# A fused adaLN block on Trainium2: in the gradient loop, upstream products are issued one batch further ahead, the slope precedes the key rates on GpSimd, and a learning rate moves from the values to the hidden product

## The chip, the cores and the metric

The kernel runs on one core of a Trainium2 chip. The metric is the device time of one launch in microseconds (us), the median of several runs. The engines are named as the profile names them: PE is TensorE (matmuls), DVE is VectorE, ACT is ScalarE, POOL is GpSimd, SP is SyncE (it only issues DMAs here). Each engine works through its own list of instructions in order; engines wait for one another on semaphores.

## The reference

One block computes, for 8 batches of 256 tokens with 256 channels (2 heads of 128), a modulated layer norm, a fast-weight attention, a residual, a second modulated layer norm, a mixture of experts and a residual. The change lies in the fast-weight attention, where each batch and head gets three gradients:

```python
qkv = silu(x @ w_qkv.T);  q, k, v = ...       # per head 256 x 128, q and k normalised
lr  = softplus(x @ w_lr.T + BASE_LR_INV)      # three rates per token and head: lr0, lr1, lr2

gate_before_act   = w0 @ kT
hidden_before_mul = w2 @ kT
silu_gate = silu(gate_before_act)
hidden    = silu_gate * hidden_before_mul
dhidden   = w1.T @ vT
dhidden_before_mul = dhidden * silu_gate
dgate = dhidden * hidden_before_mul
dgate_before_act = _silu_backprop(dgate, gate_before_act)
dw1 = vT @ (hidden.T * lr1)
dw0 = dgate_before_act @ (k * lr0)
dw2 = dhidden_before_mul @ (k * lr2)
w0, w1, w2 = zeropower(dw0) + dw0, ...        # five Newton-Schulz steps in bf16 on all 48 matrices,
                                              # each divided by its Frobenius norm first
```

## The kernel before

The program is written by hand for each engine; the order of the work is the order of the code, and every dependence is a semaphore. Its stages, by the time of the profiled execution: layer norm, QKV and normalisation of the keys (0 to 72 us), the gradient loop (72 to 118), five Newton-Schulz steps over 12 groups of four matrices (to about 197), the output of the attention batch by batch (to about 255), and the mixture of experts (to the end).

**The gradient loop** runs over b = 0 to 7 (one batch each; a batch has two token tiles, so with two heads four 128x128 blocks). Per batch:

- PE, `fast_up(b)`: the upstream products. Four times a 128x256 product `kT` with `w0` and `w2` (names `w,kT`) and a 128x128 product `vT` with `w1` (`w1s,vT`), into PSUM banks that alternate with the parity of b. It ends with `up_ps`. For b >= 2 it waits for `b_dg` of batch b - 2.
- ACT, `sigmoid(b)`: sigmoid of the gate, tile `s_` (two buffers). `scaled_values(b)`: four 128x128 products of the values with their rate lr1, tile `vl1` (two buffers).
- DVE, `gate_slopes(b)`: `sg` = gate * sigmoid, `u` = (sigmoid - 1) * sg. `gate_products(b)`: `hid` = sg * hidden, `dhb` = sg * dhidden, two buffers each. `sg` and `u` have one buffer.
- POOL, `gate_slope(b)`: `u` = sigmoid - u, the slope (semaphore `b_ds`). `key_rates(b)`: four products that scale the keys by lr0 and lr2 (`kl0`, `kl2`, two buffers).
- DVE: `dgb` = u * hidden, then times dhidden (`b_dg`).
- PE, `grads(b)`: twelve 128x128 products into banks 6 and 7, which have no second buffer: it waits for `dw_sb`, the copies of the gradients of b - 1 out of these banks. Ends with `dw_ps`.
- ACT, `grads_out(b)`: two copies of 128x384 from PSUM to `dw` (`dw_sb`).
- DVE, `cast_grads(b)`: `dw` to bf16, tile `X` (`xb_ok`). ACT, `grad_squares(b)`: six squared sums of `X` (128x128 each, name `junk`). PE, `frob_sums(b)`: one small product that adds them over the partitions. ACT, `sum_out(b)`: copies the result to `fsum`. POOL, `frobenius`: root of it (`fnb`), two batches at a time at first.

In front of `frob_sums` and `grads`, PE waits for the `dw_sb` and the `f_sum` of the step before. After the loop come `x_init` (division by the norm), the first transposes (`first_turn` on PE, `first_turned` on ACT and DVE), the inverse norms of batches 4 and 5, the cast of batch 7 and its squares `gsq` on DVE, and then the first `Br` of the Newton-Schulz loop. ACT closes the loop with the squares of batches 5 and 6, the sums, and the copy of batch 7.

Of the kernel before, what the change touches and what calls it, by code (L numbers as in the profile page):

```python
# [27 lines left out]
P = 128  # L28
# [46 lines left out]
def build(nc, x_d, c_d, wmod_d, qkvw_d, w02_d, w1_d, wnat_d, wo_d, onw_d, gate_d, ident_d, moew_d, comb_d, out_d):  # L75
    ctx = ExitStack()
    with ctx:
# [74 lines left out]
        qkvlo = at("qkvlo", [P, KC, QKV + NLR], F32R, R_dw + 8 * KC * L * 2)  # L152
        names = [(f"{n}{i}", [P, 4, P], F32) for i in range(2) for n in ("s_", "hid", "dhb", "dgb", "kl0", "kl2", "vl1")]
        tb, end = carve(R_tmp, names + [("sg", [P, 4, P], F32), ("u", [P, 4, P], F32)])
        assert end <= R_wo
        s_sb, hid, dhb, dgb, kl0, kl2, vl1 = ([tb[i], tb[7 + i]] for i in range(7))
        sg, u = tb[14], tb[15]
        gsq = at("gsq", [P, 6, P], F32, R_tmp + 14 * 2048)
# [73 lines left out]
        def bank(i):  # L232
            return banks[i // 2][:, (i % 2) * BLK:(i % 2 + 1) * BLK]
# [11 lines left out]

            "up_ps", "sig", "b_sg", "b_u", "b_ds", "b_t", "b_dg", "b_kl", "b_vl", "dw_ps", "dw_sb",
            "xb_ok", "f_ss", "g_sq", "f_s7",
# [163 lines left out]
        def _(po):  # L411
# [90 lines left out]
            for b in range(1, B):  # L502
                if b == (NBLK - 1) * 4 // TPB:
                    po.wait_ge(S["sc_l"], 4 * NH)
                key_rates(b)
                gate_slope(b)
                if b == 5:
                    frobenius(0, 1)
# [88 lines left out]
        def _(ac):  # L597
# [41 lines left out]

            def scaled_values(b):  # L640
                for t in range(b * TPB, (b + 1) * TPB):
                    for h in range(NH):
                        ac.activation(vl1[b % 2][:, (t - b * TPB) * NH + h, :], v[:, h, t, :], ACT.Copy,
                                      scale=lr[:, t, 3 * h + 1:3 * h + 2]).then_inc(S["b_vl"], 1)

            def sigmoid(b):
# [52 lines left out]
            turned_q(NBLK - 1)  # L699
            ac.wait_ge(S["lr_ok"], 1)  # L700
            scaled_values(0)

# [23 lines left out]

            for b in range(B):
                if b >= 1:
                    sigmoid(b)
                if b >= 2:  # L730
                    ac.wait_ge(S["dw_ps"], b - 1)
                if b >= 1:
                    scaled_values(b)
                if b >= 2:
                    grad_squares(b - 2, range(6) if b < B - 1 else range(3))
                if b >= 1:
                    grads_out(b - 1)
                if b >= 3:
                    sum_out(b - 3)
# [133 lines left out]
        def _(pe_):  # L873
# [126 lines left out]
            def grads(b):  # L1000
                i = b % 2
                pe_.wait_ge(S["b_dg"], b + 1)
                pe_.wait_ge(S["b_vl"], 4 * (b + 1))
                if b >= 1:
                    pe_.wait_ge(S["dw_sb"], NH * b)
                else:
                    pe_.wait_ge(S["at_sb_q"], 2 * NH)
                for h in range(NH):
                    pe_.wait_ge(S["b_kl"], 4 * b + 2 * (h + 1))
                    if b == B - 1 and h == 1:  # L1010
                        frob_sums(B - 3)
                    for j, (left, right) in enumerate(((dgb, kl0), (vl1, hid), (dhb, kl2))):
                        for tl in range(TPB):
                            last = mm(bank(6 + h)[:, j * P:(j + 1) * P], left[i][:, tl * NH + h, :], right[i][:, tl * NH + h, :],  # L1014
                                      start=(tl == 0), stop=(tl == TPB - 1))
                last.then_inc(S["dw_ps"], 1)
# [21 lines left out]
            for b in range(1, B + 1):  # L1038
                if b < B and b > 1:
                    fast_up(b)  # L1040
                if b >= 3:
                    pe_.wait_ge(S["dw_sb"], NH * (b - 1))
                    if b >= 4:
                        pe_.wait_ge(S["f_sum"], b - 3)
                    if b < B:
                        frob_sums(b - 3)
                grads(b - 1)
# [240 lines left out]
        def _(ve):  # L1288
# [77 lines left out]
            def gate_slopes(b):  # L1366

                i = b % 2
                ve.wait_ge(S["sig"], b + 1)
                if b >= 2:  # L1370
                    ve.wait_ge(S["dw_ps"], b - 1)
                if b >= 1:
# [5 lines left out]
            def gate_products(b):  # L1378

                i = b % 2  # L1380
                ve.tensor_tensor(hid[i][:, :, :], sg[:, :, :], hid_ps(i), ALU.mult)
                ve.tensor_tensor(dhb[i][:, :, :], sg[:, :, :], dh_ps(i), ALU.mult)
# [51 lines left out]
            for b in range(B):  # L1434
                i = b % 2
                if b >= 1:
                    gate_slopes(b)
                    gate_products(b)
                ve.wait_ge(S["b_ds"], b + 1)
                ve.tensor_tensor(dgb[i][:, :, :], u[:, :, :], hid_ps(i), ALU.mult).then_inc(S["b_t"], 1)  # L1440
                ve.wait_ge(S["b_t"], b + 1)
                ve.tensor_tensor(dgb[i][:, :, :], dgb[i][:, :, :], dh_ps(i), ALU.mult).then_inc(S["b_dg"], 1)
                if b >= 1:
                    cast_grads(b - 1)
            for b in range(3):
# [289 lines left out]
```

## Time and profile before

| what | value |
|---|---|
| median of 3 runs | 679.16 us (678.9 to 680.42) |
| profiled execution, its own time | 679.29 us |
| span of that execution, first to last instruction | 677.5 us |
| PE busy in the span | 651.7 us (96%) |
| DVE, ACT, POOL busy | 467.4, 339.2, 229.6 us |
| gradient loop | 72 to 118 us |

A timeline row below gives the start in us from the span's beginning, the duration in us, the engine, the line of the program, the operation, the tile written and the tiles read (buffer numbers left out), the shapes, and how many instructions were merged into it. A bracket at the end says how long the engine stood idle before it and which instruction ended that wait. A duration includes the time until the result is written; the next instruction on the engine may start a little earlier, so costs on an engine are taken from start to start.

### The profile page before, as it was taken

To read this page: it belongs to the slowest core of one execution; us is meant where nothing else is said; L and a number is where in the kernel's file an instruction comes from. 1 tells how busy PE (TensorE), PEld (TensorE's weight loads), DVE (VectorE), ACT (ScalarE), POOL (GpSimd) and SP (SyncE) were. 2 spreads that over 40 slices of the span, in tenths; PEclk is the share of its full clock that TensorE was granted. 3 is DMA by queue.
4 is the path that set the end of the run, shared out by engine and by line. 5 is a ranking of instruction groups with operands and counts; after the bars stand their busy time and mean duration, and the time that the engine had idled before them with its cause. 6 is when DMAs were issued, how large, how long until landed. Compare 5 with 4: busy or idle time off the path is not lost.

```text
span 677.5 us, 11548 instructions
## 1 busy us (share of the span) xinstructions
PE 651.7 (96%) x4146; PEld 560.6 (83%) x4146; DVE 467.4 (69%) x921; ACT 339.2 (50%) x725; POOL 229.6 (34%) x221
## 2 busy tenths in 40 slices
PE   7999998799988999999999999999999999999997
PEld 7889898799976887878888888888888888888885
DVE  6988878889977787774457665667556665555545
ACT  4788699789988855533222223322223332222331
POOL 4578868868177631340003310133002330000000
PEclk7999999999999999999999999999999999999999
DMA  8000000150000000430023422233222331122122
GB/s 327 6 1 1 1 2 3 46 174 26 3 2 0 2 1 1 121 104 25 15 86 108 107 75 69 78 117 109 63 66 86 109 117 67 62 66 69 54 94 107
DMA packets 23095, 43.58 MB, mean 64 GB/s; under 512 B 3544, under 2 KB 5856, under 8 KB 22912
## 3 DMA queue, kind: packets, MB, share of 16 engines
q1 hardware_dynamic: 22624, 42.26, 19.8%
q8 instruction: 34, 0.56, 0.4%
q10 hardware_dynamic: 416, 0.59, 0.3%
q14 instruction: 21, 0.17, 0.1%
HBM read 40.60 MB, written 2.24 MB: 63 GB/s over the span
## 4 chain that ended last, share of the span: by engine, by line
PE 78%; DVE 9%; POOL 6%; ACT 4%; issue 2%; DMA 1%; DVEq 0%; SPq 0%; ACTq 0%; POOLq 0%
PE ps L1176 40%; PE ps L1261 20%; PE ps L973 3%; PE ps L1100 2%; PE ps L1124 2%; PE ps L1111 2%; PE ps L1125 2%; PE ps L1140 2%; PE ps L1014 1%; PE ps L1222 1%; DVE x L1625 1%; PE ps L1198 1%; POOL qk L446 1%; ACT junk L725 1%; DMA x<-in_x 1%
## 5 line engine op out<-in xcount | busy, mean ns | idle before, releaser
L866 ACT ACTIVATE sgm<-ps,zero 128x512 f32<-128x512 f32 x100 | 69.0, 691 | 272.9 <-PE ps L1176 272.8
L1676 DVE TENSOR_TENSOR am<-sgm,ps 128x512 f32<-128x512 f32 x88 | 60.6, 689 | 138.9 <-ACT sgm L866 138.8
L1176 PE MATMUL ps<-h2hi,whi 128*128 128x512 f32 x400 | 156.1, 390 | 0.0
L1176 PE MATMUL ps<-h2lo,whi 128*128 128x512 f32 x400 | 155.6, 389 | 0.0
L1176 PE MATMUL ps<-h2hi,wlo 128*128 128x512 f32 x400 | 155.6, 389 | 0.0
L536 POOL CAST whi<-raw 128x768 fp32r<-128x768 f32 x25 | 23.2, 927 | 239.6 <-DMA raw<-in_moew 239.6
L1176 PEld LDWEIGHTS ps<-h2lo,whi 128*128 128x128 f32 x400 | 75.1, 188 | 15.7
L1176 PEld LDWEIGHTS ps<-h2hi,whi 128*128 128x128 f32 x400 | 75.1, 188 | 15.6
L1176 PEld LDWEIGHTS ps<-h2hi,wlo 128*128 128x128 f32 x400 | 75.1, 188 | 15.4
L1261 PE MATMUL ps<-ahi,whi 128*128 128x512 f32 x200 | 77.9, 390 | 0.1
L1261 PE MATMUL ps<-ahi,wlo 128*128 128x512 f32 x200 | 77.8, 389 | 0.0
L1261 PE MATMUL ps<-alo,whi 128*128 128x512 f32 x200 | 77.8, 389 | 0.0
L1640 DVE TENSOR_TENSOR alo<-pm,ahi 128x512 fp32r<-128x512 f32 x100 | 76.1, 761 | 0.2
L1685 DVE TENSOR_TENSOR pm<-am,cw 128x512 f32<-128x512 f32 x88 | 70.4, 800 | 5.3 <-DMA cw<-combine 2.9
L856 ACT ACTIVATE ahi<-pm 128x512 fp32r<-128x512 f32 x100 | 62.2, 622 | 2.0 <-DVE pm L1685 1.0
L538 POOL TENSOR_TENSOR wlo<-raw,whi 128x768 fp32r<-128x768 f32 x25 | 48.3, 1932 | 2.0
L1496 DVE SCALAR_TENSOR_TENSOR Br<-ps,Ar 128x512 bf16<-128x512 f32 x60 | 41.4, 691 | 6.6 <-PE ps L1111 5.6
L1261 PEld LDWEIGHTS ps<-ahi,whi 128*128 128x128 f32 x200 | 37.5, 188 | 8.3 <-DVE alo L1640 0.5
L1261 PEld LDWEIGHTS ps<-alo,whi 128*128 128x128 f32 x200 | 37.5, 188 | 7.8
L1261 PEld LDWEIGHTS ps<-ahi,wlo 128*128 128x128 f32 x200 | 37.5, 188 | 7.7
L764 ACT ACTIVATE Ar<-ps 128x512 bf16<-128x512 f32 x60 | 35.5, 594 | 5.5 <-DVE Br L1496 2.8
L772 ACT ACTIVATE X<-ps 128x512 bf16<-128x512 f32 x60 | 35.9, 599 | 2.3 <-PE ps L1125 0.5
(213 smaller groups left out, 1183.3 us busy)
## 6 DMA issues: line engine op xcount, KB each, us to landing
raw<-in_moew SPq DMA_DIRECT2D x25, 384.0 KB, 3.9
cw<-combine SPq DMA_DIRECT2D x32, 256.0 KB, 3.2
cw<-combine SPq DMA_DIRECT2D x16, 224.0 KB, 3.0
cw<-combine SPq DMA_DIRECT2D x16, 192.0 KB, 2.8
cw<-combine SPq DMA_DIRECT2D x16, 160.0 KB, 2.7
wog<-combine SPq DMA_DIRECT2D x2, 1024.0 KB, 6.3
cw<-combine SPq DMA_DIRECT2D x16, 128.0 KB, 3.0
out<-x1T SPq DMA_DIRECT2D x8, 256.0 KB, 3.6
```

The source lines that it names most:

```text
L536: po.tensor_copy(whi[wg % 2][:, c, :], raw[:, j % 2, :]).then_inc(S["w_hi"], 1)
L538: po.tensor_tensor(wlo[wg % 2][:, c, :], raw[:, j % 2, :], whi[wg % 2][:, c, :].bitcast(F32), ALU.subtract).then_inc(S["w_prep"], 1)
L764: ac.activation(Ar[:, n % 2, :], bank(n % 2), ACT.Copy, scale=NS[n // NGRP][1]).then_inc(S["a_sb"], 1)
L772: ac.activation(X[:, g * MPG:(g + 1) * MPG, :], bank(4 + n % 2).rearrange("p (a d) -> p a d", d=P), ACT.Copy).then_inc(S["x_sb"], 1)
L856: ac.activation(ahi[:, n % 4, :], pm[:, n % 3, :], ACT.Copy).then_inc(S["e_hi"], 1)
L866: ac.activation(sgm[:, n % 2, :], gate_bank(n), ACT.Silu, bias=zero[:, :]).then_inc(S["e_sg"], 1)
L1176: last = mm(o, w_, a_[:, kc, tok], start=(kc == 0 and k == 0), stop=(kc == KC - 1 and k == 2))
L1261: last = mm(bank(6 + f), w_, a_, start=(c == 0 and k == 0), stop=(c == CPG - 1 and k == 2))
L1496: ve.scalar_tensor_tensor(out=Br[:, n % 2, :], in0=bank(2 + n % 2), scalar=c_ / (b_ * b_), in1=Ar[:, n % 2, :], op0=ALU.mult, op1=ALU.add) ...
L1640: ve.tensor_tensor(alo[:, n % 3, :], pm[:, n % 3, :], ahi[:, n % 4, :].bitcast(F32), ALU.subtract).then_inc(S["e_lo"], 1)
L1676: ve.tensor_tensor(am[:, n % 2, :], sgm[:, n % 2, :], lin_bank(n), ALU.mult).then_inc(S["e_a"], 1)
L1685: ve.tensor_tensor(pm[:, n % 3, :], am[:, n % 2, :], cw[:, k % 3, :], ALU.mult).then_inc(S["e_p"], 1)
```

## The change

It does four things. (1) On PE, the loop issues `fast_up(b + 1)` ahead of `grads(b - 1)`, where it was `fast_up(b)`; so `fast_up(2)` stands ahead of `grads(0)`, and no upstream product is left in front of `grads(6)`. ACT takes the sigmoids a batch earlier in its list accordingly. (2) On POOL, from batch 1 on, `gate_slope(b)` stands ahead of `key_rates(b)`. (3) The rate lr1 is multiplied into `hid` on DVE: four 128x128 instructions with a rate per partition in place of one of 128x512. `scaled_values` and the tile `vl1` go away; PE reads the values `v` themselves. (4) On DVE the cast of a gradient moves: `cast_grads(b - 2)` between the products and `dgb` of batch b, in place of `cast_grads(b - 1)` behind them; the wait for the gradients of b - 2 moves from `sg` to `hid`.

```diff
@@ POOL @@
             for b in range(1, B):
                 if b == (NBLK - 1) * 4 // TPB:
                     po.wait_ge(S["sc_l"], 4 * NH)
+                gate_slope(b)
                 key_rates(b)
-                gate_slope(b)
@@ ACT @@
-            def scaled_values(b):
-                for t in range(b * TPB, (b + 1) * TPB):
-                    for h in range(NH):
-                        ac.activation(vl1[b % 2][:, (t - b * TPB) * NH + h, :], v[:, h, t, :], ACT.Copy,
-                                      scale=lr[:, t, 3 * h + 1:3 * h + 2]).then_inc(S["b_vl"], 1)
...
-            ac.wait_ge(S["lr_ok"], 1)
-            scaled_values(0)
+            sigmoid(1)
...
-            for b in range(B):
-                if b >= 1:
-                    sigmoid(b)
-                if b >= 2:
-                    ac.wait_ge(S["dw_ps"], b - 1)
-                if b >= 1:
-                    scaled_values(b)
+            for b in range(1, B):
+                if b + 1 < B:
+                    sigmoid(b + 1)
                 if b >= 2:
                     grad_squares(b - 2, range(6) if b < B - 1 else range(3))
                 if b >= 1:
@@ PE @@
                 pe_.wait_ge(S["b_dg"], b + 1)
-                pe_.wait_ge(S["b_vl"], 4 * (b + 1))
...
-                    for j, (left, right) in enumerate(((dgb, kl0), (vl1, hid), (dhb, kl2))):
+                    for j in range(3):
                         for tl in range(TPB):
-                            last = mm(bank(6 + h)[:, j * P:(j + 1) * P], left[i][:, tl * NH + h, :], right[i][:, tl * NH + h, :],
-                                      start=(tl == 0), stop=(tl == TPB - 1))
+                            m = tl * NH + h
+                            left, right = ((dgb[i][:, m, :], kl0[i][:, m, :]), (v[:, h, b * TPB + tl, :], hid[i][:, m, :]),
+                                           (dhb[i][:, m, :], kl2[i][:, m, :]))[j]
+                            last = mm(bank(6 + h)[:, j * P:(j + 1) * P], left, right, start=(tl == 0), stop=(tl == TPB - 1))
...
             for b in range(1, B + 1):
-                if b < B and b > 1:
-                    fast_up(b)
+                if b + 1 < B:
+                    fast_up(b + 1)
@@ DVE @@
                 ve.wait_ge(S["sig"], b + 1)
-                if b >= 2:
-                    ve.wait_ge(S["dw_ps"], b - 1)
...
-                ve.tensor_tensor(hid[i][:, :, :], sg[:, :, :], hid_ps(i), ALU.mult)
+                if b >= 2:
+                    ve.wait_ge(S["dw_ps"], b - 1)
+                if b == 0:
+                    ve.wait_ge(S["lr_ok"], 1)
+                for tl in range(TPB):
+                    for h in range(NH):
+                        m = tl * NH + h
+                        ve.scalar_tensor_tensor(out=hid[i][:, m, :], in0=hid_ps(i)[:, m, :],
+                                                scalar=lr[:, b * TPB + tl, 3 * h + 1:3 * h + 2], in1=sg[:, m, :], op0=ALU.mult, op1=ALU.mult)
...
                     gate_products(b)
+                if b >= 2:
+                    cast_grads(b - 2)
...
-                if b >= 1:
-                    cast_grads(b - 1)
+            cast_grads(B - 2)
```

The end of the loop on PE, behind the gradients of batch 5 (`kl`, `hid` and `dhb` of odd batches are numbered 88 to 92 before and 87 to 90 in the change, of even ones 81 to 85). Before, the upstream products of the last batch follow (two of eight rows shown):

```order
L1014 MATMUL ps<-kl_91,dgb_90 128x128 x2
L1014 MATMUL ps<-hid_88,vl_93 128x128 x2
L1014 MATMUL ps<-kl_92,dhb_89 128x128 x2
L942 MATMUL ps<-w_124,kT 128x256
L944 MATMUL ps<-w1s,vT 128x128
```

In the change:

```order
L1005 MATMUL ps<-kl_90,dgb_89 128x128 x2
L1005 MATMUL ps<-hid_87,v 128x128 x2
L1005 MATMUL ps<-kl_91,dhb_88 128x128 x2
L987 MATMUL ps<-fss,ones 128x6
L1005 MATMUL ps<-kl_84,dgb_83 128x128 x2
L1005 MATMUL ps<-hid_81,v 128x128 x2
```

The upstream products have moved ahead of the gradients of batch 5; behind these, the norm sum of batch 4 and the gradients of batch 6 follow at once.

One batch on DVE (batch 2, buffers `s_80`, `hid_81`, `dhb_82`, `dgb_83`), before:

```order
L1374 TENSOR_TENSOR sg<-s_80,ps 128x512
L1376 SCALAR_TENSOR_TENSOR u<-s_80,sg 128x512
L1381 TENSOR_TENSOR hid_81<-sg,ps 128x512
L1382 TENSOR_TENSOR dhb_82<-sg,ps 128x512
L1440 TENSOR_TENSOR dgb_83<-u,ps 128x512
L1442 TENSOR_TENSOR dgb_83<-dgb_83,ps 128x512
L1415 CAST X<-dw 128x768
```

and in the change:

```order
L1362 TENSOR_TENSOR sg<-s_80,ps 128x512
L1364 SCALAR_TENSOR_TENSOR u<-s_80,sg 128x512
L1376 SCALAR_TENSOR_TENSOR hid_81<-ps,lr,sg 128x128 x4
L1378 TENSOR_TENSOR dhb_82<-sg,ps 128x512
L1411 CAST X<-dw 128x768
L1438 TENSOR_TENSOR dgb_83<-u,ps 128x512
L1440 TENSOR_TENSOR dgb_83<-dgb_83,ps 128x512
```

`hid` has become four instructions, and the cast (now of the gradient two batches back) stands between the products and `dgb`.

## Rows read from the trace of the kernel before

**Rows 1.** Busy time by window: us, engines' busy us, PE clock, DMA

```profile
72.00:118.00 46.00, 41.69 (x319) 39.34 (x317) 37.56 (x61) 39.93 (x144) 36.05 (x44) 1.00 0.01 1
```

**Rows 2.** PE's timeline, batches 0 to 3: start, duration, instructions, idle before

```profile
74.66 0.68 PE L1014 MATMUL ps<-kl,dgb 128*128 128x128 f32 x4 [1.60 <-DVE dgb L1442]
...
77.41 0.60 PE L942 MATMUL ps<-w,kT 128*128 128x256 f32 x2
...
80.03 0.62 PE L1014 MATMUL ps<-kl,dgb 128*128 128x128 f32 x4
...
82.72 0.60 PE L942 MATMUL ps<-w,kT 128*128 128x256 f32 x2
...
86.18 0.69 PE L1014 MATMUL ps<-kl,dgb 128*128 128x128 f32 x4
...
91.58 0.36 PE L998 MATMUL ps<-fss,ones 128*128 128x6 f32 x2
91.85 0.68 PE L1014 MATMUL ps<-kl,dgb 128*128 128x128 f32 x4
```

**Rows 3.** PE's timeline at the loop's end

```profile
114.26 0.68 PE L1014 MATMUL ps<-kl,dgb 128*128 128x128 f32 x4 [1.90 <-DVE dgb L1442]
...
117.23 0.83 PE L1034 MATMUL ps<-identb,X 128*128 128x128 bf16 x12
```

**Rows 4.** DVE's timeline, from the rates to the first gradient product

```profile
71.78 0.26 DVE L1409 SCALAR_TENSOR_TENSOR lr<-lrp,lrz 128x96 f32<-128x96 f32 x1
71.96 0.68 DVE L1381 TENSOR_TENSOR hid<-sg,ps 128x512 f32<-128x512 f32 x1
...
73.87 0.69 DVE L1442 TENSOR_TENSOR dgb<-dgb,ps 128x512 f32<-128x512 f32 x1
```

**Rows 5.** Groups of DVE by form: busy us, mean ns of one

```profile
L1625 DVE SCALAR_TENSOR_TENSOR x<-ps,rr,x 128x256 f32<-128x256 f32 x32 | 13.7, 478 | 3.6 <-POOL rr L581 2.6 <-PE ps L1222 1.0
...
L1440 DVE TENSOR_TENSOR dgb<-u,ps 128x512 f32<-128x512 f32 x8 | 5.5, 688 | 3.2 <-POOL u L484 3.2
...
L1531 DVE TENSOR_TENSOR ex<-ps,mx 128x128 f32<-128x128 f32 x2 | 0.6, 291 | 0.1
```

**Rows 6.** DVE's timeline: four such instructions in a row, in the output stage

```profile
215.53 1.66 DVE L1625 SCALAR_TENSOR_TENSOR x<-ps,rr,x 128x256 f32<-128x256 f32 x4 [1.38 <-POOL rr L581]
```

**Rows 7.** DVE's timeline, batches 3, 4 and 6

```profile
91.45 0.56 DVE L1415 CAST X<-dw 128x768 bf16<-128x768 f32 x1 [0.74 <-ACT dw L717]
92.48 0.69 DVE L1374 TENSOR_TENSOR sg<-s,ps 128x512 f32<-128x512 f32 x1 [0.47 <-ACT s L651]
...
95.29 0.69 DVE L1440 TENSOR_TENSOR dgb<-u,ps 128x512 f32<-128x512 f32 x1 [0.20 <-POOL u L484]
...
109.16 0.77 DVE L1415 CAST X<-dw 128x768 bf16<-128x768 f32 x1
```

**Rows 8.** ACT's timeline: batch 4, and the sum of batch 5

```profile
91.76 0.69 ACT L651 ACTIVATE s<-ps,zero 128x512 f32<-128x512 f32 x1 [0.28 <-PE ps L944]
92.35 1.27 ACT L643 ACTIVATE vl<-v,lr 128x128 f32<-128x128 f32 x4
93.52 0.39 ACT L725 ACTIVATE junk<-X,zero 128x128 f32<-128x128 bf16 x1
...
96.56 0.85 ACT L717 ACTIVATE dw<-ps 128x384 f32<-128x384 f32 x2
97.30 0.17 ACT L705 ACTIVATE fsum<-ps 128x6 f32<-128x6 f32 x1
...
116.33 0.15 ACT L705 ACTIVATE fsum<-ps 128x6 f32<-128x6 f32 x1
```

**Rows 9.** POOL's timeline: the key rates of batch 4

```profile
89.22 2.34 POOL L478 TENSOR_TENSOR kl<-qk,lr 128x256 f32<-128x256 f32 x4
```

**Rows 10.** DVE's timeline: the last cast and the first Br

```profile
119.81 0.52 DVE L1415 CAST X<-dw 128x768 bf16<-128x768 f32 x1
...
122.73 0.67 DVE L1496 SCALAR_TENSOR_TENSOR Br<-ps,Ar 128x512 bf16<-128x512 f32 x1
```

More of the change, by code:

```diff
@@ L152, in build @@
         qkvlo = at("qkvlo", [P, KC, QKV + NLR], F32R, R_dw + 8 * KC * L * 2)
-        names = [(f"{n}{i}", [P, 4, P], F32) for i in range(2) for n in ("s_", "hid", "dhb", "dgb", "kl0", "kl2", "vl1")]
+        names = [(f"{n}{i}", [P, 4, P], F32) for i in range(2) for n in ("s_", "hid", "dhb", "dgb", "kl0", "kl2")]
         tb, end = carve(R_tmp, names + [("sg", [P, 4, P], F32), ("u", [P, 4, P], F32)])
         assert end <= R_wo
-        s_sb, hid, dhb, dgb, kl0, kl2, vl1 = ([tb[i], tb[7 + i]] for i in range(7))
-        sg, u = tb[14], tb[15]
+        s_sb, hid, dhb, dgb, kl0, kl2 = ([tb[i], tb[6 + i]] for i in range(6))
+        sg, u = tb[12], tb[13]
         gsq = at("gsq", [P, 6, P], F32, R_tmp + 14 * 2048)
@@ L244, in build @@
             "lr_z", "lr_e", "lr_c", "lr_ok",
-            "up_ps", "sig", "b_sg", "b_u", "b_ds", "b_t", "b_dg", "b_kl", "b_vl", "dw_ps", "dw_sb",
+            "up_ps", "sig", "b_sg", "b_u", "b_ds", "b_t", "b_dg", "b_kl", "dw_ps", "dw_sb",
             "xb_ok", "f_ss", "g_sq", "f_s7",
```

## The prediction

> **What bounds the kernel now.** I read busy time by window first, then the timelines of PE, DVE and ACT in the window that the change touches. Outside 72 to 118 us no instruction changes, and the stages behind the loop follow one another without a fixed appointment, so the change is worth what it moves the start of the Newton-Schulz loop. I date that by the first `Br` on DVE, 122.73 us [rows 10], since it is held up there by the casts and squares of the last batches.
>
> In the window PE is busy 41.69 of 46 us [rows 1], so at most 4.3 us can be had, and that only if PE never waits. Its waits are mainly two: 1.60 us ahead of the first gradients [rows 2] and 1.90 us ahead of the last [rows 3], both for `dgb` of that batch. Between them PE is nearly full: a batch without a wait (gradients, upstream products, norm sum) takes 86.18 to 91.85 = 5.67 us [rows 2], and 39.6 us lie between the start of the first gradients (74.66) and that of the last (114.26), which is 5.66 per batch. The middle of the loop therefore has almost nothing to give. DVE does wait in every batch (0.74 for the copy of the gradient, 0.47 for the sigmoid, 0.20 for the slope [rows 7]), but those waits lie behind PE's 5.67.
>
> **The change part by part.**
>
> *Rate into hid, the head of the loop.* Before, `hid` started at 71.96, before the rates were written; now it must wait for them: 71.78 + 0.26 = 72.04, so 0.08 us [rows 4]. Then four 128-column instructions with a rate per partition replace one of 512. The trace has the same form at 256 columns: 478 ns for one [rows 5], four in 1.66 us, so (1.66 - 0.478)/3 = 0.394 from start to start [rows 6]. A column costs (688 - 291)/384 = 1.03 ns [rows 5]; 128 fewer columns leave 0.262 from start to start and 0.346 for one alone. The lower end is the rates' own instruction, 96 columns without PSUM: its successor starts 0.18 later [rows 4], with 32 more columns 0.21. I take 0.262, the nearest form: four are 1.05 in place of 0.60 (`hid`, `dhb` and the first `dgb` take 1.91 together, the last 0.71 with the wait for its result [rows 4]), so +0.45 (bounds +0.24 and +0.78). `dgb` of batch 0, and with it PE's start, comes 0.53 later (0.32 to 0.86): 74.66 + 0.53 = 75.19. In later batches the 0.45 lies behind PE (below).
>
> *PE's order.* What is called a batch further ahead is in its waits only a swap: `fast_up(b + 1)` and `grads(b - 1)` both wait for `dgb` of b - 1. From 75.19: `fast_up(2)` 2.62 (77.41 to 80.03) and 0.06 for a start from idle (gradients 2.75 after a wait, 2.69 without), gradients of 0 2.69, up(3) and gradients of 1 5.31, to 85.87; three batches of 5.67, to 102.88; up(7) 2.62, to 105.50; sum 0.27 and gradients of 5 2.75, to 108.52 [rows 2]. That needs the others to keep up. DVE: `sg` to `dgb` 2.81 less the wait 0.20 and the old `hid` 0.60 [rows 7], plus 1.05, cast 0.56, twice `dgb` 1.44: 5.06 us, or 5.27 with the cast at 0.77 [rows 7]: under 5.67, and its waits for the sigmoid and the slope find them done, since the sigmoid comes a batch earlier and the slope's place in POOL's list ahead of the key rates lets it run under `hid` and `dhb`. ACT: sigmoid 0.59, squares 3.04, copies 0.74, sum 0.12 [rows 8], 4.5. POOL: 36.05 us in the window [rows 1] is 4.5 per batch. So PE is full from 75.19 to 108.52, and the middle gains what it waited there: 4.3 less 1.6 and 1.9, some 0.8 us in all.
>
> *Values' rate gone from ACT.* Four instructions, 92.35 to 93.52 = 1.17 us per batch [rows 8], eight batches. ACT is not the bound, so this is worth nothing by itself; it pays only by making ACT's 4.5 fit under 5.67.
>
> *The end of the loop.* Here the swap costs. Before, up(7) stood between the gradients of 5 and of 6 and covered ACT's copies out of banks 6 and 7, which have no second buffer. Now nothing stands there. ACT's list is sigmoid(7), six squares, copies of 5, sum. The sigmoid starts 0.18 after PE leaves the products (91.58 to 91.76 [rows 2, 8]): 105.68; squares from 106.27 to 109.31; copies to 110.05; sum 0.17; PE goes on at about 110.3 (0.1 for the handover). It has waited 1.8 us. Sum and gradients of 6 to 113.3; copies from 113.47 to 114.21, sum, PE at 114.48: another 1.2 us, where before it was 1.90 for `dgb`. The gradients of 7 take 2.97 (114.26 to 117.23 [rows 3]), to 117.45, 0.2 later than before. ACT, free of copies at 114.33, still has three squares of batch 5 and three of 6 (1.52 each, half of 3.04) before the sum of batch 5: 117.37, where it was at 116.33 [rows 8]. Behind that sum hang the root on POOL, the inverse norms and, queued behind these on DVE, the cast of batch 7, its squares and the first `Br` [rows 10]. All of it moves by **+1.04 us** (0.83 to 1.37 with the bounds of `hid`).
>
> The sum is made against the profiled execution's own 679.29 us, of which 677.5 is span: 680.33. That execution lies 0.13 above the median of 679.16, so the median comes to **680.2**.
>
> *A rule weighed.* A cast on DVE and key rates on POOL disturb each other: 0.56 us in one place, 0.77 in another where POOL works [rows 7]. The Trainium skill (SBUF — State Buffer, "Who interferes with whom") says more: the two engines share a port pair as a lock, a cast can take it, and whoever comes second blocks until the other's whole instruction is done. In the change each cast lies over key rates. By the rows this adds 0.21 under PE's cover and nothing to the sum; by the rule as it stands a cast could lose a whole POOL instruction, which is the second rival; the rows so far show a third of one.
>
> **The rivals.**
>
> 1. *The forecast:* the middle gains 0.8, the head loses 0.53, the single-buffered banks give the rest back. 680.2, by its bounds 680.0 to 680.5.
>
> 2. *VectorE becomes the bound (slower).* `hid` at its upper end, 1.38, and each cast behind a whole key-rate instruction, 2.34/4 = 0.59 [rows 9]: 2.01 + 1.38 + 0.56 + 0.59 + 1.44 = 5.98 per batch against PE's 5.67. It decides from a DVE batch of 5.67 on. Six batches of 0.31 are 1.9, the head costs 0.33 more: 1.04 + 1.9 + 0.33 = +3.3, 682.4. For it: VectorE gets longer in a loop that is nearly full. Against: it takes both upper ends; one alone gives 5.39 or 5.65.
>
> 3. *VectorE alone sets what follows (faster).* It leaves the loop early: `hid` of batch 7 may start when the gradients of 5 are done (108.7); 1.05, 0.60, cast 0.56, `dgb` 1.44 give 112.3, where before PE got the last `dgb` at 114.26 [rows 3]. If the divisions by the norms could start then, all would come 1.9 earlier: 677.3. Against: the cast of batch 6 now stands ahead of them and waits for copies that end at 114.2.
>
> **How the numbers follow.** A measurement of this kernel can tell about 0.2% (1.36 us) from no change. The runs before spread over 1.5 us, so a median may be off by half a microsecond, beside the bounds of `hid` and of ACT's tail. The forecast gets 0.83: 0.58 within 0.2%, 0.24 above it, 0.01 below. VectorE as the bound gets 0.09 (slower), VectorE alone 0.08 (faster). So faster 0.09, same 0.58, slower 0.33. The range runs from 679.1 to 681.6: it holds the forecast's bounds with about a microsecond on either side, and leaves out both rivals and a little of the forecast's tails.
>
> **What would show it.** In the changed profile: PE's first upstream product of the loop after a wait at about 75.2; PE without a wait from there to about 108.5, a batch at 5.6 to 5.7; then two waits, about 1.8 and 1.2, ended by ACT's copy or sum and no longer by `dgb`; `hid` four at about 0.26 from start to start; DVE's waits now for the gradients' end ahead of `hid`; the first `Br` at about 123.8. The prediction is wrong if PE waits for `dgb` in the middle (rival 2), if the two late waits are missing or ACT's sum of batch 5 comes before 116.3 (rival 3), or if the `Br` moves and the end does not move with it.

## The result, and the profile after

The changed kernel takes 683.38 us (median of 15 runs, 679.98 to 685.0) against 680.83 us (15 runs of the kernel before, 677.73 to 682.88, taken beside them): a ratio of 1.0033, 95% interval 1.0021 to 1.0045, or +2.25 us (+1.4 to +3.1) by that ratio; the medians themselves lie 2.55 apart. In a second group of runs it was 682.13 against 680.43, ratio 1.0020 (1.0005 to 1.0034), +1.4 us. It is slower, the forecast of no measurable change was wrong, and 683.38 lies outside the range of 679.1 to 681.6.

The profiled execution of the changed kernel took 679.98 us, its fastest, with a span of 678.0. By the end of the span it would be only 0.5 us slower than the profile of before. That comparison is of no use here: from the first `Br` to the end, where no instruction differs, the two profiles of the kernel before took 554.8 and 557.3 us. Ahead of the loop the two executions differ as well, with no change there: from 8 to 16 us the granted clock of TensorE was 0.57 in the profile of before and 1.00 in that of the changed kernel. So I read everything from a point just ahead of the change to a point just behind it: from the start of the rates (the instruction that writes `lr` on DVE) to the first `Br`. The same measure is used for every kernel below.

Busy time by window (us, busy us of PE, weight loads, DVE, ACT, POOL, then PE's clock, DMA share, GB/s) of the kernel after; [rows 1] answer to the first line:

```profile
72.00:118.00 46.00, 40.86 (x300) 38.76 (x300) 39.93 (x82) 28.84 (x103) 35.12 (x43) 0.96 0.01 1
...
72.00:82.00 10.00, 7.77 (x45) 7.03 (x45) 8.36 (x18) 1.37 (x2) 5.98 (x10) 0.83 0.01 2
...
76.00:77.00 1.00, 1.00 (x4) 0.82 (x4) 1.00 (x5) 0.00 (x0) 0.69 (x1) 0.50 0.00 0
```

ACT lost 11 us of its 40, as the removal of the scaled values wants, and DVE gained 2.4. The new thing is the clock: 1.00 over the whole stretch before, 0.96 now, and all of the loss lies in the first 10 us. PE's timeline of the kernel after shows where; [rows 2] answer:

```profile
74.87 0.67 PE L931 MATMUL ps<-w,kT 128*128 128x256 f32 x2 [2.23 <-DVE dgb L1440]
75.37 0.56 PE L933 MATMUL ps<-w1s,vT 128*128 128x128 f32 x2
75.73 1.06 PE L931 MATMUL ps<-w,kT 128*128 128x256 f32 x2
76.58 0.63 PE L933 MATMUL ps<-w1s,vT 128*128 128x128 f32 x2
...
79.23 0.61 PE L1005 MATMUL ps<-kl,dgb 128*128 128x128 f32 x4
...
89.97 0.69 PE L1005 MATMUL ps<-kl,dgb 128*128 128x128 f32 x4
...
95.49 0.69 PE L1005 MATMUL ps<-kl,dgb 128*128 128x128 f32 x4
```

PE waits 2.23 us for the first `dgb` where it waited 1.60, and half a microsecond into the upstream products behind it the pairs of matmuls stretch from 0.60 to 1.06 us: the granted clock is 0.50 there (the row from 76 to 77 us above), the 1.2 GHz level; it is back at 1.00 from 79 us on. Such a drop to the lower level is called a fall below. `fast_up(2)` takes 74.87 to 79.23 = 4.36 us in place of 2.62. From there on PE is full: a batch takes 89.97 to 95.49 = 5.52 us.

DVE at the head of the loop, kernel after ([rows 4] answer):

```profile
71.39 0.26 DVE L1405 SCALAR_TENSOR_TENSOR lr<-lrp,lrz 128x96 f32<-128x96 f32 x1
71.68 1.13 DVE L1376 SCALAR_TENSOR_TENSOR hid<-ps,lr,sg 128x128 f32<-128x128 f32 x4
72.72 0.68 DVE L1378 TENSOR_TENSOR dhb<-sg,ps 128x512 f32<-128x512 f32 x1
```

Four `hid` to the start of `dhb`: 1.04 us, as priced. PE at the end of the loop ([rows 3] answer), ACT's sum of batch 5 ([rows 8]), a cast in the middle ([rows 7]), and the first `Br` ([rows 10]), all of the kernel after:

```profile
111.22 0.36 PE L987 MATMUL ps<-fss,ones 128*128 128x6 f32 x2 [1.75 <-ACT fsum L698]
115.52 0.68 PE L1005 MATMUL ps<-kl,dgb 128*128 128x128 f32 x4 [1.16 <-ACT fsum L698]
118.54 0.83 PE L1024 MATMUL ps<-identb,X 128*128 128x128 bf16 x12
```

```profile
118.30 0.15 ACT L698 ACTIVATE fsum<-ps 128x6 f32<-128x6 f32 x1
```

```profile
89.21 1.01 DVE L1411 CAST X<-dw 128x768 bf16<-128x768 f32 x1
...
124.75 0.68 DVE L1493 SCALAR_TENSOR_TENSOR Br<-ps,Ar 128x512 bf16<-128x512 f32 x1
```

From the rates' start (71.39) to the first `Br` (124.75) it is 53.36 us; before it was 122.73 - 71.78 = 50.95. The window of the change costs 2.41 us. Two theories were open. **Clock theory:** 1.7 us of it come from the fall of the clock behind PE's wait at the head of the loop, which the change made longer, and only the rest from the order of the work. **Schedule theory:** the order costs all of it, and the clock is incidental or hidden.

### The profile page after: what moved, and what is told of

Same layout as the page of the kernel before. It is cut to its first block, busy times and chain, and to the rows that moved or that the text cites. A ratio compares the mean times of both kernels' runs of the same rounds, so it can differ in the third digit from the quotient of the medians.

```text
span 678.0 us, 11532 instructions
## 1 busy us (share of the span) xinstructions
PE 653.9 (96%) x4146; PEld 563.2 (83%) x4146; DVE 473.2 (70%) x945; ACT 329.1 (49%) x693; POOL 229.3 (34%) x221
## 4 chain that ended last, share of the span: by engine, by line
PE 81%; DVE 7%; POOL 5%; ACT 4%; issue 2%; DMA 1%; SPq 0%; DVEq 0%; ACTq 0%; POOLq 0%
PE ps L1166 40%; PE ps L1251 20%; PE ps L962 2%; PE ps L1005 2%; PE ps L1114 2%; PE ps L1090 2%; PE ps L1101 2%; PE ps L1115 2%; PE ps L931 2%; PE ps L1130 2%; PE ps L1212 1%; DVE x L1622 1%; PE ps L1188 1%; PE ps L933 1%; ACT junk L718 1%
## 5 line engine op out<-in xcount | busy, mean ns | idle before, releaser
L1637 DVE TENSOR_TENSOR alo<-pm,ahi 128x512 fp32r<-128x512 f32 x100 | 77.7, 777 | 0.2
L1682 DVE TENSOR_TENSOR pm<-am,cw 128x512 f32<-128x512 f32 x88 | 71.9, 817 | 5.2 <-DMA cw<-combine 2.8
```

Source lines behind the costliest of these rows:

```text
L1637: ve.tensor_tensor(alo[:, n % 3, :], pm[:, n % 3, :], ahi[:, n % 4, :].bitcast(F32), ALU.subtract).then_inc(S["e_lo"], 1)
L1682: ve.tensor_tensor(pm[:, n % 3, :], am[:, n % 2, :], cw[:, k % 3, :], ALU.mult).then_inc(S["e_p"], 1)
```

## The experiments

Each diff is against the kernel that the text names. Below, "rates to Br" is the measure just described, from each kernel's own profile. In the expectations the fall of the clock is always priced from the 4.36 against 2.62 us above.

**The changed kernel with PE kept busy ahead of the loop.** (The expectation says 512 columns; the extra matmuls have 128.)

```diff
             pe_.wait_ge(S["ident_ok"], 1 + NS_STEPS)
+            pe_.wait_ge(S["at_sb_q"], 2 * NH)
+            spin(9)
             for b in range(1, B + 1):
```

> The changed kernel with nine extra matmuls of 512 columns on PE whose product nobody reads, ahead of the loop and behind the last attention products that PE turns: PE is busy for most of the time in which it otherwise waits for the first dgb. No instruction of another engine changes. Clock theory: the first upstream products of the loop run at the upper clock (about 2.6 us where the changed kernel showed 4.36), so the kernel is about 1.7 us faster than the changed one: +0.5 to +1.0 us against before. Schedule theory (the lower clock there is incidental or hidden): no difference from the changed kernel, +2.2 us against before.

Measured: 680.49 us, ratio to before 0.9995 (0.9977 to 1.0014), where the changed kernel itself has 1.0033 and 1.0020. PE's timeline of this kernel:

```profile
72.35 2.17 PE L877 MATMUL ps<-ones 128*128 128x128 f32 x18
74.70 0.67 PE L931 MATMUL ps<-w,kT 128*128 128x256 f32 x2 [0.18 <-DVE dgb L1442]
75.21 0.38 PE L933 MATMUL ps<-w1s,vT 128*128 128x128 f32 x2
75.43 0.60 PE L931 MATMUL ps<-w,kT 128*128 128x256 f32 x2
...
77.39 0.61 PE L1005 MATMUL ps<-kl,dgb 128*128 128x128 f32 x4
```

DVE's rates and first `Br`, ACT's sum of batch 5, and the row of the window behind the loop, of the same kernel:

```profile
71.22 0.26 DVE L1407 SCALAR_TENSOR_TENSOR lr<-lrp,lrz 128x96 f32<-128x96 f32 x1
...
122.93 0.67 DVE L1495 SCALAR_TENSOR_TENSOR Br<-ps,Ar 128x512 bf16<-128x512 f32 x1
```

```profile
116.48 0.15 ACT L698 ACTIVATE fsum<-ps 128x6 f32<-128x6 f32 x1
```

```profile
118.00:125.00 7.00, 4.37 (x51) 3.58 (x52) 6.42 (x10) 4.78 (x13) 6.60 (x5) 0.86 0.33 109
```

`fast_up(2)` now takes 74.70 to 77.39 = 2.69 us. Rates to Br is 122.93 - 71.22 = 51.71, 1.65 less than in the changed kernel, though useful work starts no sooner. In this stretch matmuls that compute nothing win back 1.65 us, as the clock theory wants, and what the order itself costs is 51.71 - 50.95 = 0.76 us. But this execution has a fall too: the clock is at the lower level from 123.0 us on (0.86 from 118 to 125, where both kernels without the extra matmuls have 1.00), 0.1 us behind the `Br` that ends the measure, and no wait of PE in the 9 us ahead of that was longer than 0.9 us. So the measure shows what a fall inside it costs, and not that the extra matmuls rid an execution of falls. That they win time over whole executions rests on the ratio of the 12 runs; its interval lies clear of the changed kernel's first one (1.0021 to 1.0045) and overlaps a little with its second (1.0005 to 1.0034), both taken in other groups.

**A control: the kernel before, filled the same way.**

```diff
             pe_.wait_ge(S["ident_ok"], 1 + NS_STEPS)
+            pe_.wait_ge(S["at_sb_q"], 2 * NH)
+            spin(6)
             for b in range(1, B + 1):
```

> The kernel before with six extra matmuls of 128 columns on PE ahead of the loop, whose product nobody reads; its wait there falls from 1.6 to about 0.2 us. A control for the filled changed kernel. Clock theory: before loses nothing to the clock there, so filling gives nothing: -0.3 to +0.3 us. If filling helps by itself, whatever the wait (for instance by what it does to the clock later on): about -2 us here too.

Measured: 680.83 us, ratio 1.0000 (0.9984 to 1.0016). Filling by itself gives nothing in time. In its profile the clock had fallen ahead of the loop (0.72 from 66 to 72 us), PE came late, and the matmuls overshot: rates to Br 51.93.

**The rate into hid alone, on the kernel before.** Orders unchanged, so the first work behind PE's wait is gradients.

```diff
-                ve.tensor_tensor(hid[i][:, :, :], sg[:, :, :], hid_ps(i), ALU.mult)
+                if b == 0:
+                    ve.wait_ge(S["lr_ok"], 1)
+                for tl in range(TPB):
+                    for h in range(NH):
+                        m = tl * NH + h
+                        ve.scalar_tensor_tensor(out=hid[i][:, m, :], in0=hid_ps(i)[:, m, :],
+                                                scalar=lr[:, b * TPB + tl, 3 * h + 1:3 * h + 2], in1=sg[:, m, :], op0=ALU.mult, op1=ALU.mult)
...
-                    scaled_values(b)
```

> The kernel before with only the rate moved: four hid instructions with a rate per partition on VectorE, the scaled values gone from ACT, gradients read v itself; all orders stay. Schedule theory: ACT is relieved by 1.17 us per batch and the head loses 0.5 us; together -0.5 to +0.3 us against before. Clock theory: PE's first wait in the loop grows from 1.6 to about 2.1 us as in the changed kernel, the granted clock falls behind it, the first gradients take some 1.5 to 1.8 us longer, and the kernel is 1 to 1.5 us slower than before.

Measured: 681.82 us, ratio 1.0013 (0.9995 to 1.0031): inconclusive in time. PE's timeline:

```profile
75.19 0.68 PE L1010 MATMUL ps<-kl,dgb 128*128 128x128 f32 x4 [2.18 <-DVE dgb L1443]
...
76.69 1.06 PE L1010 MATMUL ps<-kl,dgb 128*128 128x128 f32 x4
77.55 1.06 PE L1010 MATMUL ps<-hid,v 128*128 128x128 f32 x4
...
115.42 0.68 PE L1010 MATMUL ps<-kl,dgb 128*128 128x128 f32 x4 [2.18 <-DVE dgb L1443]
115.94 0.61 PE L1010 MATMUL ps<-hid,v 128*128 128x128 f32 x4
```

The longer `hid` brings the longer wait, and a fall follows it here too, with gradients behind the wait in place of upstream products. Rates to Br is 52.13, +1.18; if the fall costs 1.65 here too, the edit by itself gives 0.5 us back. That it does so through the work that ACT no longer has is not shown. But the last wait of the same execution, also 2.18 us, has no fall behind it. The length of a wait alone doesn't decide.

**The order alone, on the kernel before.**

```diff
-                if b < B and b > 1:
-                    fast_up(b)
+                if b + 1 < B:
+                    fast_up(b + 1)
```

with the sigmoid moved a batch earlier on ACT, as in the change.

> The kernel before with only PE's order changed: upstream products of b+1 ahead of the gradients of b-1, and the sigmoid a batch earlier on ACT to match. The scaled values stay on ACT, hid stays one 512-column instruction, GpSimd's and VectorE's orders stay. Schedule theory: ACT still carries 1.17 us of scaled values per batch and the end of the loop loses the cover of its copies out of banks 6 and 7, so the order alone, without relief for ACT, costs several us: 682 to 686 where before is 680.8. Clock theory: the first wait of PE in the loop stays at about 1.6 us, so the granted clock stays at the upper level behind it and whatever is lost is lost to waits only. Rival (the order is harmless): within 1 us of before.

Measured: 688.78 us, ratio 1.0115 (1.0089 to 1.0141), +7.8 us; rates to Br is 132.78 - 72.78 = 60.00. DVE, then PE:

```profile
89.60 0.56 DVE L1416 CAST X<-dw 128x768 bf16<-128x768 f32 x1 [2.27 <-ACT dw L718]
...
96.03 0.56 DVE L1416 CAST X<-dw 128x768 bf16<-128x768 f32 x1 [1.75 <-ACT dw L718]
```

```profile
94.43 0.67 PE L943 MATMUL ps<-w,kT 128*128 128x256 f32 x2 [1.19 <-DVE dgb L1443]
...
116.49 0.56 PE L999 MATMUL ps<-fss,ones 128*128 128x6 f32 x2 [2.92 <-ACT fsum L706]
116.91 1.20 PE L1015 MATMUL ps<-kl,dgb 128*128 128x128 f32 x4
117.91 1.06 PE L1015 MATMUL ps<-hid,vl 128*128 128x128 f32 x4
```

With 1.17 us of scaled values still on ACT and the cast where it was, DVE waits 1.3 to 2.3 us for ACT's copies in each batch and PE waits for `dgb`, which the full change avoids. So the other parts together make the swap bearable; which of them does it is not shown. At the end the clock falls again, half a microsecond before a wait of 2.92 us ends (0.50 from 116.0 us on); the expectation of no fall in this kernel was wrong there, for it looked at the head alone.

**A longer head wait in the kernel before,** by one repeated `dhb` on DVE.

```diff
+            ve.tensor_tensor(dhb[0][:, :, :], sg[:, :, :], dh_ps(0), ALU.mult).then_inc(S["spare"], 1)
+            ve.wait_ge(S["spare"], 1)
             gate_products(0)
```

> The kernel before with one instruction of VectorE repeated ahead of the loop (the product dhb of batch 0, 0.72 us with the wait for its result): the first dgb and with it PE's first gradients come 0.7 us later, nothing else changes. Schedule theory: +0.7 us or less, since the loop still waits elsewhere. Clock theory: PE's wait there grows from 1.6 to 2.3 us, the granted clock falls behind it, the first gradients or products take 1.5 to 1.8 us longer, and the whole is +1.5 to +2.4 us.

Measured: 681.83 us, ratio 1.0013 (0.9993 to 1.0033): inconclusive. In its profile the clock fell ahead of the loop, PE came late, and its wait was 0.81 us in place of the wanted 2.3; rates to Br is 51.62, +0.67 for the 0.72 us put in, with no fall in the loop.

**The head as before, in the changed kernel.** Batch 0 alone has the old `hid` and scaled values.

```diff
                 if b == 0:
-                    ve.wait_ge(S["lr_ok"], 1)
-                for tl in range(TPB):
+                    ve.tensor_tensor(hid[i][:, :, :], sg[:, :, :], hid_ps(i), ALU.mult)
+                for tl in range(TPB) if b else ():
```

> The changed kernel with batch 0 alone treated as in the kernel before: its hid is one 512-column instruction ahead of the rates, and ACT scales the values of batch 0. All later batches and all orders as changed. dgb of batch 0 then comes about 0.5 us earlier and PE's first wait in the loop falls from 2.2 to about 1.6 to 1.7 us. Clock theory: at that length the granted clock stays up, as it did in the kernel before, so the first upstream products take 2.6 us in place of 4.36 and the kernel gains 0.5 + 1.7 = 2.2 us on the changed one (about 0 against before). Schedule theory (the clock has no part in it): 0.5 us gained on the changed one, +1.7 against before. Third possibility: the clock falls behind a wait of 1.6 us too where upstream products follow it in place of gradients; then also only 0.5 us.

Measured: 681.51 us, ratio 1.0008 (0.9994 to 1.0022), +0.5 us (-0.4 to +1.5): between the two expectations, and just short of the +1.7 of the schedule theory. Rates to Br 51.13, without a fall, again in an execution in which PE came late (75.44 to 75.56, a wait of 0.12 us), so it doesn't tell what 1.6 us would have done. It does show the price of the four `hid`: 51.71 - 51.13 = 0.58 us.

**Both kernels a second time, and three extra matmuls in place of nine** (the edit of the filled kernel with `spin(3)`).

> The changed kernel as it stands, a second time, beside the others of this group. Clock theory: PE waits about 2.2 us ahead of the loop and the clock falls behind it again, unless the clock has already fallen in the last 6 us ahead of the loop, as the profiles of four other kernels showed: then PE comes late, its wait is under 1 us and no fall follows. Time +1.5 to +2.8 us against before. If the clock at the loop's head is incidental: no fall in this profile although PE waits 2.2 us.

> The kernel before a second time, for its profile alone. If its clock falls in the last 6 us ahead of the loop (a late PE), its first Br lies about 1.2 to 1.5 us later than in the first profile, at 124.0 to 124.3; otherwise as in the first, wait 1.6, first gradients at full clock, Br 122.7.

> The changed kernel with three extra matmuls ahead of the loop in place of nine: PE's wait there is 1.5 us, about that of the kernel before, in place of 2.2 or 0.2. Clock theory, with the wait of the kernel before short enough: as with nine, -1.5 to -2.5 us on the changed kernel (0 to +0.7 against before). If any wait over 1 us lets the clock fall: little gained.

Measured: the changed kernel 682.13 us, ratio 1.0020 (1.0005 to 1.0034). PE's timeline in this execution, head and end of the loop:

```profile
75.74 0.67 PE L931 MATMUL ps<-w,kT 128*128 128x256 f32 x2 [2.20 <-DVE dgb L1440]
76.25 0.38 PE L933 MATMUL ps<-w1s,vT 128*128 128x128 f32 x2
76.47 0.60 PE L931 MATMUL ps<-w,kT 128*128 128x256 f32 x2
...
110.44 0.36 PE L987 MATMUL ps<-fss,ones 128*128 128x6 f32 x2 [1.77 <-ACT fsum L698]
...
111.79 1.06 PE L1005 MATMUL ps<-kl,dhb 128*128 128x128 f32 x4
112.64 1.06 PE L1005 MATMUL ps<-kl,dgb 128*128 128x128 f32 x4
```

At the head this is what the expectation had named as the sign of an incidental clock: a wait of 2.20 us and no fall. A fall came behind the wait of 1.77 us at the end instead, which the expectation did not have. That wait is new too; it is one of the two that the uncovered copies make. Rates to Br is 53.35, the same as in the first profile (53.36) to 0.01 us: one fall cost the same at these two places. The kernel before went as in its first profile: waits of 1.62 and 1.91, no fall, 50.94 against 50.95. With three extra matmuls the time was 681.99, ratio 1.0019 (1.0003 to 1.0035), only 0.1 us under the changed kernel beside it: over the runs they won nothing, which is the side of the rival ("little gained"). Its profile, late again ahead of the loop, has 51.72 and no fall in the loop. It shows the 0.77 of the schedule once more, but what a wait of 1.5 us does there it leaves open.

Two profiles say little of all the executions; their mean granted clocks are on record. In this group they average 0.9909 for the changed kernel (12 runs), 0.9910 with three extra matmuls (12) and 0.9927 for the kernel before (23). The fall at 75 us takes 1.7 us off the first profile's 678 (0.28, 0.50, 0.50 and 0.43 in the four microseconds from 75 on), which is 0.0025. So I estimate that an execution of the changed kernel has 0.7 falls more than one of before, give or take 0.6 by the scatter of the runs (95%). The kernel with nine extra matmuls has 0.9929 (12 runs) against 0.9912 for the kernel before beside it (29), so no more falls than before.

**The end of the loop altered, alone and with everything.** The gradients of batch 6 get banks of their own; ACT copies ahead of squaring; the norm sums move behind the gradients.

```diff
+        def grad_bank(b, h):
+            return bank((0, 4)[h] if b == B - 2 else 6 + h)
...
-                    grad_squares(b - 2, range(6) if b < B - 1 else range(3))
+                    grad_squares(b - 2, range(6) if b < B - 1 else range(1))
...
-                    if b < B:
-                        frob_sums(b - 3)
+                    frob_sums(b - 3)
...
+                if b == B - 1:
+                    pe_.wait_ge(S["dw_sb"], NH * (b - 1))
+                    pe_.wait_ge(S["f_sum"], b - 3)
+                    frob_sums(b - 3)
```

> The changed kernel with the end of the loop only altered: the gradients of batch 6 go to PSUM banks 0 and 4 (free by then) so that they need not wait for ACT's copies of batch 5, the norm sums of batches 4 to 6 move behind the gradients they stood before, and ACT copies the gradients of batches 6 and 7 ahead of the squares. The head is as changed, so the clock may fall there as in the changed kernel. Theory of the uncovered copies: PE's two waits of 1.75 and 1.16 us go or become one shorter wait for dgb of batch 7, gradients of batch 7 end some 2.5 us earlier, ACT's squares and the divisions by the norms then take over, first Br 1.5 to 2 us earlier: 1.5 to 2 us gained on the changed kernel (+0.3 to +0.8 against before). Rival (the end of the loop is set by ACT's or VectorE's queue whatever PE does): under 0.5 us gained.

> The changed kernel with batch 0 as before, five extra matmuls of 128 columns ahead of the loop whose product nobody reads, and the altered end of the loop. Clock theory and uncovered copies both: 2.2 + 1.8 = 4.0 us gained on the changed kernel, -1.5 to -2 us against before (679 or less). If only one of them is right, about 0 against before.

Measured: alone 681.53 us, ratio 1.0003 (0.9987 to 1.0020); rates to Br 51.91, so 1.45 us gained on the changed kernel's 53.36, near the 1.5 to 2 expected. That is with the fall at the head still in it (wait 2.22) and with a second one that the alteration brought, from 119.6 us on, in a wait of 2.28 us for ACT among the turns (clock 0.62 from 118 to 125 us). With the head of before and five extra matmuls too: 679.21 us, ratio 0.9976 (0.9961 to 0.9991), 1.6 us faster than before; rates to Br 120.84 - 71.53 = 49.31. This is what was expected if both losses are real and can be had back. The new long wait among the turns is there again, and the clock fell from 120.4 us on (of the kernel with everything, PE's row and the row of the window):

```profile
118.25 0.61 PE L1033 MATMUL ps<-identb,X 128*128 128x128 bf16 x8 [2.56 <-ACT XT L710]
```

```profile
118.00:125.00 7.00, 5.94 (x66) 5.17 (x66) 6.12 (x10) 5.12 (x12) 6.57 (x5) 0.76 0.00 0
```

**That wait split in two,** by ACT's order: the first turned group, then the gradients of batch 7, then most squares of batch 6.

```diff
             sum_out(B - 3)
-            grad_squares(B - 2, range(1, 3))
-            grads_out(B - 1)
-            grad_squares(B - 2, range(3, 6))
+            grad_squares(B - 2, range(1, 2))
             first_turned(0)
+            grads_out(B - 1)
+            grad_squares(B - 2, range(2, 4))
             first_turned(2)
+            grad_squares(B - 2, range(4, 6))
```

> The kernel with the head of before, the extra matmuls and the altered end of the loop, with one thing more: ACT copies the first turned group out of PSUM and the gradients of batch 7 ahead of most squares of batch 6, so that PE's one wait of 2.3 to 2.6 us among the turns, behind which the clock fell, is split into two of about 1 us. VectorE's chain up to the first Br is unchanged. Clock theory: no fall between 118 and 125 us, 0.3 to 0.8 us gained, -2 to -2.5 us against before. If what follows the loop is set by VectorE alone: no difference, -1.6.

Measured: 678.54 us, ratio 0.9957 (0.9944 to 0.9971), 2.9 us faster than before: the best of all. Its reason isn't the one expected. The wait is split (PE):

```profile
116.81 0.62 PE L1034 MATMUL ps<-identb,X 128*128 128x128 bf16 x8 [1.03 <-DVE X L1443]
118.69 0.36 PE L996 MATMUL ps<-fss,ones 128*128 128x6 f32 x2 [1.26 <-ACT junk L725]
```

but the clock from 118 to 125 us is 0.76 as without the split: it falls from 120.5 us on, behind waits of 1.03 and 1.26 us. Rates to Br is 49.33 against 49.31. What lowers its median by 0.7 us more lies behind the first `Br` or in executions that no profile shows; the two intervals overlap, and this is left open.

## Why the prediction was wrong

**The step that failed** is the one that runs PE on from 75.19 with "`fast_up(2)` 2.62". It took the duration from [rows 2], where it had been measured behind a shorter wait and at a clock of 1.00, and put it behind a wait that the same paragraph had just lengthened. The rows of before held no fall in the loop ([rows 1], clock 1.00); the lower level was in its trace from 8 to 16 us only. What could have been seen is that the sum made PE's wait at the head longer and added two new ones at the end, and gave none of them a chance of a lower clock. What the runs showed in its place is a fall that costs 53.36 - 51.71 = 1.65 us in this stretch. Both profiles of the changed kernel have one, one at the head and one at the end of the loop; neither profile of before has any there. That the longer waits bring it is made likely by the filled kernel, and is not settled (below). As a rival it would have given 680.2 + 1.65 = 681.9 on the prediction's own base.

**The schedule** was right in its parts, a little too dear in its sum: 0.76 us (51.71 and 51.72 in the two profiles without a fall in this stretch, against 50.95 and 50.94) for a forecast of 1.04.

- Head: PE's start moved by 0.60 against the rates (74.70 - 71.22 = 3.48, before 74.66 - 71.78 = 2.88); forecast 0.53. The four `hid` are 1.04, forecast 1.05.
- Middle: full as forecast, at 5.52 us per batch in place of 5.67. The term that was mis-sized is the norm sum: it takes 0.14 where PE doesn't wait ahead of it, not the 0.27 of [rows 2].
- End: waits of 1.75 and 1.16, ended by ACT's sum behind the copies, forecast 1.8 and 1.2. No wait for `dgb`.
- ACT's sum of batch 5, by the filled kernel's row at 116.48, 45.26 behind the rates; before 116.33 - 71.78 = 44.55. So +0.71 for a forecast of +1.04, the difference being the shorter batches.

**VectorE as the bound** did not come about: in the middle DVE waits for PE again (about half a microsecond at most ahead of `hid`), although casts beside GpSimd's products took up to 1.01 us in place of 0.55. That is a loss of 0.46, twice what [rows 7] had shown, but less than the whole 0.59 that this rival charged. In the kernel with the head of before one cast took 1.18 us, a loss of 0.63, so the rival's price for a cast does occur. The Trainium skill (SBUF — State Buffer, "Who interferes with whom") would let a cast lose a whole GpSimd instruction; the rows agree in kind, and in size the 0.63 comes up to a whole key-rate instruction while most casts lose less. All of it lay behind PE. **VectorE alone** fell with the two waits and with the `Br` that came later, not sooner.

**The base** was low as well. The three runs shown had a median of 679.16; over 15 runs it is 680.83. A median of three executions that scatter over 5 us carries more than the half microsecond that I allowed. With the right base and the forecast of +1.04 the time would be 680.83 + 1.04 = 681.9, still 1.5 us short; the missing fall is 1.65. Sized by what was measured, the sum is 680.83 + 0.76 + 1.65 = 683.24 against 683.38, if each execution has one fall more than before. In the second group, with 0.7 of a fall by the estimate above, it is 0.76 + 0.7 * 1.65 = 1.9 us for a measured +1.4 (+0.3 to +2.3). One of the signs of being wrong that the prediction names did show in the profile: the `Br` moved by 124.75 - 122.73 = 2.02 us and the end of the span by 0.5. Over the runs the end did move, and what hid it in the two profiles is the scatter of the part behind the `Br` (553.2 against 554.8 us).

**What stays open.** In 14 profiles PE waited 8 times for 2.18 us or longer in or just behind the loop. In three of these cases the clock fell 0.4 to 1.3 us after PE had gone on, in two (the 2.28 and the 2.92) half a microsecond before the wait ended, behind the 2.56 it fell 2.1 us after, and behind two it stayed. Of the 11 waits from 1.60 to 1.94 one was followed by a fall, and that one was in the changed kernel. By these counts longer waits bring more falls, but a fall needs none of them: two came with no wait over 1.3 us in the 9 us ahead of them (at 120.5 in the split kernel, at 123.0 in the filled one). In five of the 14 the clock fell at about 68 us, ahead of the loop, in kernels whose work is the same there; PE had been busy for 11.89 of the 12 us from 56 to 68, and no wait stands ahead of these falls. What decides a single case no run here settles. That the longer waits, and not chance, put the falls into the changed kernel's loop rests on two profiles of each kernel, on the mean clocks and on the filled kernel's time. The Trainium skill (TensorE: Matmul & The Clock Gate, "What's actually happening") says that the chip's look at the engine's activity runs free and isn't started with the kernel, so that the same kernel changes clock at different points in different runs. The fall at 75 us in one execution of the changed kernel and at 111 us in the other agrees; no run here moves that start by itself.

## What to carry to other kernels

Where a change lengthens PE's longest wait or adds new ones of one to three microseconds, add to the sum the chance that the clock falls behind them: here a fall cost 1.65 us, twice the whole schedule. Matmuls that compute nothing, put into the wait, are a cheap test of it: nine of them brought the time back to that of before, three did not. And when an order is turned round, look at the end of the loop, where the work that used to cover a single-buffered copy is missing; second banks that are free by then, and copies ahead of other work, brought 1.45 us back here.

## What the runs showed of the hardware that was not expected

The granted clock can fall at a single wait of 1.77 to 2.9 us: in four cases 0.4 to 1.3 us after PE had gone on, as in the rows at 75.37 and 111.79, and in two before the wait ended, so that the first matmul is slow already (116.49, 0.56 in place of 0.36). The same wait in the same program is followed by a fall in one execution (2.23 us, at the head) and not in another (2.20 us). A cast of 768 columns on DVE took 0.55 us alone and up to 1.18 us beside GpSimd's products. And the part of this program that no change touches varied by 4.3 us between 13 profiles (553.2 to 557.5 from the first `Br` to the end). Falls have a share in that: the six profiles with one from 268 to 270 us on took 555.3 to 557.5, the seven others 553.2 to 556.0. So an effect of 2 us must be read between two points around the change.
